# Normalised activations stored with a pair's channels slow and the pixels fast: the first transform of a two-layer convolution kernel loads its weights from consecutive words

## The reference

```python
# layer 0: decorrelated batch normalisation over all 50176 pixels
f  = x_flat - mean                                   # (64, n)
ff = (1 - EPS) * (f @ f.T / (n - 1)) + EPS * eye(64)
L  = cholesky(ff)
out = (solve_triangular(L, eye(64)) @ f) * gamma + beta
# layer 1: Fourier filter block
h = layer_norm(x, n1_g, n1_b)
xf = rfft2(h, axes=(1, 2), norm='ortho')             # 56 x 29 spectrum per channel
# 8 blocks of 8 channels: complex 8x8 product, relu, complex 8x8 product, softshrink
y = irfft2(...)
h = y + h + residual
residual = h
h = gelu(layer_norm(h, n2_g, n2_b) @ mw1 + mb1) @ mw2 + mb2
return h + residual
```

## Time and profile before

| what | value |
|---|---|
| runs of the kernel before | 1067.75, 1069.26, 1069.82 us, median 1069.26 |
| profiled execution, span on the core | 1067.7 us |
| PE / weight load / DVE / ACT / POOL busy | 949.2 / 817.9 / 719.9 / 558.1 / 272.1 us |
| chain that ended last, by engine | PE 57%, DVE 16%, ACT 14%, issue 8%, DMA 4% |

### The profile page before, as it was taken

The page is one execution under the profiler, slowest core; times in us unless marked ns, Lnnn a source line. Parts: engine busy times, 40 slices in busy tenths (PEclk is TensorE's granted clock), DMA queues, the critical chain, the costliest instruction groups (busy, mean ns, idle before and its releaser), DMA issues.

```text
span 1067.7 us, 18451 instructions
## 1 busy us (share of the span) xinstructions
PE 949.2 (89%) x6263; PEld 817.9 (77%) x6263; DVE 719.9 (67%) x2061; ACT 558.1 (52%) x1139; POOL 272.1 (25%) x107
## 2 busy tenths in 40 slices
PE   6989963887999999999999999999998999799787
PEld 6976553685689768976897689768976998499465
DVE  4456786189767776777676767676886688543762
ACT  0002011763776577657765776577647753775333
POOL 2000004034422332233223322332233224230110
PEclk8985565988999999999999999999999999989889
DMA  9922002011000300030003000200000000000001
GB/s 270 261 67 61 1 0 61 1 34 28 1 19 18 83 5 17 17 85 2 17 17 84 3 17 17 87 1 17 17 27 1 19 27 19 0 27 18 18 26 36
DMA packets 9956, 40.78 MB, mean 38 GB/s; under 512 B 1232, under 2 KB 1232, under 8 KB 8208
## 3 DMA queue, kind: packets, MB, share of 16 engines
q1 hardware_dynamic: 9888, 40.00, 13.4%
HBM read 27.15 MB, written 12.85 MB: 37 GB/s over the span
## 4 chain that ended last, share of the span: by engine, by line
PE 57%; DVE 16%; ACT 14%; issue 8%; DMA 4%; DVEq 0%; SPq 0%; ACTq 0%
PE psum L1024 13%; PE psum L909 9%; PE psum L1009 7%; PE psum L962 7%; ACT p_y L1112 7%; ACT o_g L1121 4%; PE psum L943 4%; PE psum L983 4%; PE psum L897 3%; PE psum L836 3%; DMA n<-x_dram 2%; DVE o_g L285 2%; PE psum L884 2%; DVE hbuf L568 2%; DVE stats L527 2%
## 5 line engine op out<-in xcount | busy, mean ns | idle before, releaser
L1153 ACT ACTIVATE hid<-psum,hbias 128x448 f32<-128x448 f32 x224 | 136.2, 634 | 132.2 <-PE psum L1009 131.5
L1024 PEld LDWEIGHTS psum<-prm,hid 128*112 128x112 f32 x1792 | 187.1, 182 | 8.5 <-ACT hid L1153 4.6
L1024 PE MATMUL psum<-prm,hid 128*112 128x96 f32 x1792 | 191.3, 267 | 2.3 <-ACT hid L1153 2.3
L354 POOL TENSOR_TENSOR hbuf<-hbuf,prm 112x1792 f32<-112x1792 f32 x15 | 63.3, 4217 | 328.4 <-DVE hbuf L595 328.4
L644 DVE TENSOR_TENSOR n2T<-psum,n2T 64x448 fp32r<-64x448 f32 x112 | 69.7, 622 | 102.5 <-ACT n2T L1145 101.3
L382 POOL TENSOR_TENSOR p_y<-over,under 116x512 f32<-116x512 f32 x64 | 77.2, 1208 | 201.7 <-ACT under L1171 201.6
L1009 PE MATMUL psum<-n2T,mw1h 128*128 128x448 f32 x224 | 101.8, 455 | 26.4 <-DVE n2T L644 12.8
L909 PEld LDWEIGHTS psum<-cst,hbuf 112*112 112x112 f32 x512 | 99.8, 286 | 20.5 <-issue 19.6
L909 PE MATMUL psum<-cst,hbuf 112*112 112x116 f32 x512 | 99.4, 358 | 18.1 <-DVE hbuf L777 18.1
L962 PE MATMUL psum<-cst,p_y 116*128 116x224 f32 (+1 forms) x480 | 102.1, 356 | 3.0 <-POOL p_y L382 3.0
L1100 ACT COPY u_r<-psum 112x464 f32<-112x464 f32 x64 | 35.0, 547 | 119.8 <-PE psum L909 119.8
(11 more groups left out here) (115 smaller groups left out, 1713.1 us busy)
## 6 DMA issues: line engine op xcount, KB each, us to landing
xin<-x_dram SPq DMA_DIRECT2D x9, 1568.0 KB, 8.9
out_dram<-oslice SPq DMA_DIRECT2D x56, 224.0 KB, 2.2
ybuf<-x_dram SPq DMA_DIRECT2D x2, 1568.0 KB, 18.9
fbuf<-x_dram SPq DMA_DIRECT2D x2, 1568.0 KB, 22.4
n<-x_dram SPq DMA_DIRECT2D x2, 1568.0 KB, 25.5
xin<-x_dram SPq DMA_DIRECT2D x4, 392.0 KB, 5.3
prm<-params_dram SPq DMA_DIRECT2D x1, 771.5 KB, 26.3
cst<-consts_dram SPq DMA_DIRECT2D x1, 652.0 KB, 18.9
```

The lines of the kernel that those rows point to most:

```text
L354: nc.gpsimd.tensor_tensor(h, h, row("b1", WP), ALU.add).then_inc(h_ready, 1)
L1024: last = nc.tensor.matmul(t[0:ROWS, at:at + 96], hid[:, m, w % 2, (w // 2) * ROWS:(w // 2 + 1) * ROWS], pp("mw2")[:, 128 * m + zeros:128 * ...
L1153: nc.scalar.activation(hid[:, q % 2, q // 2, :], ring_c[k % RING_C][:, 0:4 * ROWS], ACT.Gelu, bias=hbias[:, q % 2:q % 2 + 1]).then_inc(c_a ...
```

## The change

The activations of a pixel are kept in the order (j, h) instead of (h, j) in `ybuf`, `rbuf`, `fbuf`, `n2` and `p_y`: channel j stands beside channel 32 + j. `hbuf` alone is turned: (j, w, h), so that `dft_h` reads 112 consecutive numbers. The permutation is brought in by the columns of the whitening matrix `wy` and taken out where `ev_mlp` writes `oslice`; parameters are permuted on the host (`mix`). What reads or writes `hbuf` changes its access pattern:

- `ln1_subtract` reads `ybuf` in order and writes `hbuf` in pairs (h = 0, 1) that lie 448 bytes apart.
- `ln1_rstd`, `ln1_gain` and `bias_h` go through `hbuf` in 32 runs of 56 numbers; their second operand repeats in pairs.
- `residual` on POOL reads `hbuf` in pairs, the other operands in order.
- `ev_mlp` reads `fbuf` with a step of two numbers (8 bytes), 512 numbers each.
- `shrunk_sum` on POOL writes `p_y` with a step of 8 bytes instead of runs of 32 numbers.

```diff
-        h_w = h_nat.rearrange("p (m j) -> p m j", j=CH)
+        h_w = h_nat.rearrange("p (j m) -> p j m", j=CH)
+        h_tok = h_nat.rearrange("p (j w h) -> p w j h", j=CH, h=2)
...
+        def half_h(k):
+            return h_nat.rearrange("p (j w h) -> p j w h", j=CH, h=2)[:, :, k * WP:(k + 1) * WP, :]
+        def row_h(name):
+            return pp(name, ROWS).rearrange("p (j h) -> p j h", h=2).unsqueeze(2).broadcast_to((ROWS, CH, WP, 2))
...
-                        nc.gpsimd.tensor_tensor(h, h, row("b1", WP), ALU.add).then_inc(h_ready, 1)
+                        nc.gpsimd.tensor_tensor(h, h, row_h("b1"), ALU.add).then_inc(h_ready, 1)
...
-                    nc.gpsimd.tensor_tensor(r3, h3, y3, ALU.add).then_inc(r_ready, 1)
+                    nc.gpsimd.tensor_tensor(r4, h_tok, y4, ALU.add).then_inc(r_ready, 1)
...
-                        yk = y_v[0:2 * KR, 4 * k:4 * k + L2_KP[k], :].rearrange("p k (m h j) -> p h k m j", h=2, j=CH)[:, half]
+                        yk = y_v[0:2 * KR, 4 * k:4 * k + L2_KP[k], :].rearrange("p k (m j h) -> p h k m j", h=2, j=CH)[:, half]
...
-                    link(nc.vector.tensor_copy(wy[0:C, 0:C], wt_ps))
-                    link(nc.vector.tensor_copy(wy[C:2 * C, C:2 * C], wt_ps))
+                    for v in range(2):
+                        link(nc.vector.tensor_copy(
+                            wy[C * v:C * v + C, C * v:C * v + C].rearrange("p (j h) -> p h j", h=2),
+                            wt_ps.rearrange("p (h j) -> p h j", h=2)))
...
                 def ln1_subtract(i, k):
-                    subtract_mean(ybuf, h_nat, 0, k)
+                    ws = slice(k * WP, (k + 1) * WP)
+                    nc.vector.tensor_tensor(h_tok[:, ws], ybuf[:].rearrange("p (w j h) -> p w j h", j=CH, h=2)[:, ws],
+                                            small[:, 0, ws].unsqueeze(2).unsqueeze(2).broadcast_to((ROWS, WP, CH, 2)),
+                                            ALU.subtract).then_inc(norm_step[0], 1)
                 def ln1_rstd(i, k):
-                    multiply_rstd(h_nat, i, 0, k).then_inc(norm_step[0], 1)
+                    dve.wait_ge(norm_step[0], norm_count(i, 0, 2 * k + 1))
+                    nc.vector.tensor_tensor(half_h(k), half_h(k),
+                                            small[:, 3, k * WP:(k + 1) * WP].unsqueeze(1).unsqueeze(3).broadcast_to((ROWS, CH, WP, 2)),
+                                            ALU.mult).then_inc(norm_step[0], 1)
...
-                    return nc.vector.tensor_tensor(half_w(h_nat, k), half_w(h_nat, k), row("g1", WP), ALU.mult)
+                    return nc.vector.tensor_tensor(half_h(k), half_h(k), row_h("g1"), ALU.mult)
...
-                    nc.vector.tensor_tensor(oslice[:, s % 2, :], ring_c[k % RING_C][0:ROWS, :],
-                                            fbuf[:, s * SW * C:(s + 1) * SW * C], ALU.add).then_inc(c_dve, 1)
+                    nc.vector.tensor_tensor(
+                        oslice[:, s % 2, :].rearrange("p (w h j) -> p w h j", h=2, j=CH),
+                        ring_c[k % RING_C][0:ROWS, :].rearrange("p (w h j) -> p w h j", h=2, j=CH),
+                        fbuf[:, s * SW * C:(s + 1) * SW * C].rearrange("p (w j h) -> p w h j", h=2, j=CH),
+                        ALU.add).then_inc(c_dve, 1)
...
-                            last = nc.tensor.matmul(t[0:ROWS, j * 2 * KR:(j + 1) * 2 * KR], h_w[:, :, 4 * k + j],
+                            last = nc.tensor.matmul(t[0:ROWS, j * 2 * KR:(j + 1) * 2 * KR], h_w[:, 4 * k + j, :],
                                                     cc("f1", ROWS), start=True, stop=True)
```

More of the change, by code:

```diff
@@ L344, in _ @@
                 nc.gpsimd.memset(u_r[:], 0.0).then_inc(s_ones, 1)
-                h3, y3, r3, f3 = (t.rearrange("p (w c) -> p w c", c=C) for t in (h_nat, ybuf[:], r_nat, fbuf[:]))
+                f3 = fbuf[:].rearrange("p (w c) -> p w c", c=C)
+                y4, r4 = (t.rearrange("p (w j h) -> p w j h", j=CH, h=2) for t in (ybuf[:], r_nat))
                 def bias_h(i):
                     for k in range(1 if first(i) else 2):
-                        h = h3[:, k * WP:(k + 1) * WP]
+                        h = half_h(k)
                         pool.wait_ge(n1_ready, i * 2 + k + (1 if first(i) else 0))
-                        nc.gpsimd.tensor_tensor(h, h, row("b1", WP), ALU.add).then_inc(h_ready, 1)
+                        nc.gpsimd.tensor_tensor(h, h, row_h("b1"), ALU.add).then_inc(h_ready, 1)
                 def residual(i):
@@ L776, in first_h @@
                     dve.wait_ge(h0_step, 1)
-                    nc.vector.tensor_tensor(half_w(h_nat, 1), half_w(h_nat, 1), row("b1", WP), ALU.add).then_inc(h0_half, 1)
+                    nc.vector.tensor_tensor(half_h(1), half_h(1), row_h("b1"), ALU.add).then_inc(h0_half, 1)
                 covariance_and_factor()
@@ L1304, in rows, with mix @@
         return np.broadcast_to(v.reshape(1, -1), (128, v.size))
+    def mix(v):
+        return v.reshape(2, CH, -1).transpose(1, 0, 2).reshape(v.shape)
     G = CH // BS
@@ L1321, in layout @@
     put("w2", a.reshape(128, -1))
-    put("mw1", np.tile(i["L1_conv_mw1"], (2, 1)))
+    put("mw1", np.tile(mix(i["L1_conv_mw1"]), (2, 1)))
     m = np.zeros((HH, 2, 128), np.float32)
@@ L1325, in layout @@
     put("mw2", m)
[L1326 to L1329, removed]
+    put("beta", rows(mix(i["L0_conv_beta"])))
+    put("g1", rows(mix(i["L1_conv_n1_g"])))
+    put("b1", rows(mix(i["L1_conv_n1_b"])))
+    put("mb2", rows(mix(i["L1_conv_mb2"])))
     fb2 = i["L1_conv_b2"].reshape(2, 2, CH).transpose(1, 0, 2)
@@ L1332, in layout @@
     put("gamma", i["L0_conv_gamma"].reshape(C, 1))
-    put("g2", np.tile(i["L1_conv_n2_g"], 2).reshape(128, 1))
-    put("b2", np.tile(i["L1_conv_n2_b"], 2).reshape(128, 1))
+    put("g2", np.tile(mix(i["L1_conv_n2_g"]), 2).reshape(128, 1))
+    put("b2", np.tile(mix(i["L1_conv_n2_b"]), 2).reshape(128, 1))
     fb1 = i["L1_conv_b1"].reshape(2, 2, CH).transpose(0, 2, 1)
```

## The result

The changed kernel took 1029.9 us in the median of 4 runs (1024.93 to 1037.10), the kernel before 1069.5 (1067.75 to 1071.48): a ratio of 0.9632 with a 95% interval of 0.9591 to 0.9674. The profiled execution is the slowest of the four: its span is 1035.2 us. It lost 4.5 us before the first row transform (start at 183.85 instead of 179.32): the covariance's loads, where the change does nothing, left it 5.8 us late, of which it got 1.3 back. From there to the end it is 37.0 us shorter than the one of before.

What follows compares the result with a forecast made beforehand. PE bounds the step, busy 100.92 of 106.52 us. Gains of 2.8 (pair 0), 3 x 5.5 and 4 x 4.0 make 35.3; 1069.3 - 35.3 + 1.2 (clock) = 1035.2, predicted 1035, range 1024 to 1048.

Steps and rivals of the forecast that it cites:

- The load is what makes the stage long, and the stage is on the path: Row transform on PE: weight loads fall from 286 to about 180 ns, the 12.23 us stage lying wholly on the path.
- The spacing: Row transform's matmuls: 105.5 ns each instead of 191, bounds 98 to 110, saving 5.5 us per pair.
- Pair 0: First pair's row transform: nothing saved in the half at low clock, 2.8 us saved in the rest.
- DVE gives back in pairs 2 to 5 and not in 1, 6 and 7: PE's wait before mlp grows to about 2.7 us; pairs 2 to 5 gain 4.0 us each, the others 5.5.
- The patterns cost nothing: New access patterns on DVE and POOL: operations keep their times, a gain excluded; upper end on hbuf 1.1 us each.
- The rule on adjacent pairs: Skill page's rule: hbuf pairs free, single words in ev_mlp cost 0.35 us; as rival 7 us, 1042, chance 0.15 or 0.08: 0.08.
- The clock: Before mlp in pairs 2 to 5: half a fall, 1.2 us; rival of several falls, 1044, chance 0.15.

Runs made afterwards that it cites:

- pe_only: Kernel before, only the row transform changed to read consecutive numbers from the unturned hbuf (wrong numbers transformed): 1033.5 us, ratio 0.9681.
- patterns_only: Changed kernel, its row transform reading with a step of 32 numbers again, the new patterns on DVE and POOL kept: 1064.7 us, ratio 0.9977.
- late_load: Changed kernel, the input load of pair i+2 issued only when ACT has evicted the row transform of pair i: 1018.3 us, ratio 0.9557.
- single_words: Changed kernel, DVE's first normalising operation going through h before j, writing hbuf in single words 448 bytes apart: 1041.4 us, ratio 0.9760.

## Why the prediction was right, point by point

- *The load is what makes the stage long, and the stage is on the path.* Right, and shown by `pe_only` and `patterns_only`, which split the change: 0.968 and 0.998.
- *The spacing.* Predicted 105.5 ns on the line between L1024's 98 and L897's 110; measured 99, inside the bounds but near the lower. So the stage saved 5.9 instead of 5.5 us, 2.8 us more over seven pairs if all of it were kept. The straight line between L1024 and L897 was the weak step: L897's 110 ns come from 8 matmuls alone. Why the transform lies so near to L1024 no run separates.
- *Pair 0.* Predicted 2.8, measured 12.57 - 9.52 = 3.05 in the stage and 3.9 in the step. At the low clock nothing was saved, as assumed: 6.35 us for 33 matmuls before, 6.06 for 31 after, 192 and 196 ns each. That the size fits is partly luck, since it hangs on when the clock rises: in the second profile of the changed kernel the stage takes 8.70 us.
- *DVE gives back in pairs 2 to 5 and not in 1, 6 and 7.* Right: PE's wait grew from 1.32 to 2.49 us in those four (I had put 2.7), and was 1.32 and 1.17 in pairs 1 and 6. Without a fall of the clock these steps gained 4.2 and 4.7, where I had 4.0. `late_load` shows the cause: with DVE's issue time down from 6.3 to 2.0 us each step keeps 6.0 us. Two things I had otherwise. The loss has a second place, the wait of `whiten` for `ev_whiten` (0.83 us in pair 2, 0.48 in pair 4). And what DVE gives back isn't fixed: it follows the issue time one for one. Wherever the clock held, a step's gain and DVE's issue time in it add up to the same: 4.2 + 6.67 and 4.7 + 6.18 here, 5.1 + 5.68 and 3.9 + 6.97 in the second profile, 10.8 to 10.9 us each time. In `pe_only` they add up to 10.7, which is the patterns' 0.14.
- *The patterns cost nothing.* Right for all: 2.03, 2.02 (the median, which leaves the two beside POOL's bias out) and 2.03 us on `hbuf`, 687 ns for `ev_mlp`, POOL's `residual` 7.84. What I excluded, a gain, exists on POOL, 0.8 us an operation, but is worth only 0.14 us a step.
- *The rule on adjacent pairs.* Of the Trainium skill's section "Measured stream behaviour on trn2" (Vector Engine (DVE) Microarchitecture Reference) this case shows one half: pairs that hop are free (2026 ns), single words that hop cost 0.71 ns each (3297). The other half it doesn't bear out: a source stepping by 8 bytes costs nothing (`ev_mlp`, 687 ns against 689 before). `ev_mlp` also reads PSUM, at 1.3 ns an element against the 1.13 of `hbuf`'s operations, which could hide a part of such a price; but L505 reads no PSUM and shows none either. In `single_words` the source steps by 8 bytes as well, so that its 0.71 ns are the price of both together. My weighing of L505 against the rule held.
- *The clock.* I allowed half a fall, 1.2 us, and said that rows can't tell. The profile has two at the place I named, 2.2 and 3.3 us of gain left in those steps. With the issue times of these pairs (7.00 and 6.34) the sum above would have left 3.9 and 4.5 at full clock, so the falls cost 1.6 and 1.2 us, below my 2.5 to 3.4, since the clock was down for 3.4 us and not for 6.8. A second profile of the changed kernel has two as well, in pairs 2 and 5 (1.3 and 1.2 us). Which pair is hit differs between two profiles of one kernel, with the same wait of 2.49 us before it in pairs without a fall.

Sum of the profile: 3.9 + 5.9 + 14.4 + 6.1 + 6.7 = 37.0 us against the 34.1 I had forecast with the clock in. Pair 0 gave 1.1 more, pairs 1, 6 and 7 together 2.2 more. Pairs 2 to 5 gave 14.4 against my 14.8, where two errors met: gains larger than I had put, and two falls of the clock for the half that I had. The rest of the way to 1029.9 is the spread of the runs (12 us from the fastest to the slowest), of which the part ahead of the first transform moved the profiled one by 4.5 us.

What exactly DVE waits for at its loop's end the waits don't name, but the DMA packets in the traces nearly do. In every one of these waits there is one packet of 8 KB on the instruction queue q14 behind which DVE starts (times in us):

| profile, pairs | DVE's wait | from the wait's start to the packet's | from its landing to DVE's start |
|---|---|---|---|
| before, 2 to 5 (load running) | 6.5 to 7.0 | 4.3 to 4.8 | 1.7 |
| changed, 2 to 5 (load running) | 6.2 to 7.0 | 4.0 to 4.8 | 1.7 to 1.8 |
| changed, 6 (no load) | 2.0 | 0.1 | 1.4 |
| `late_load`, 2 to 6 (load later) | 2.0 to 2.2 | 0.1 | 1.5 to 1.6 |

So DVE starts at a nearly fixed time after that packet, and with the load under way the packet comes some 4 us later. That it holds DVE's own instructions, and that it queues behind the load's packets, is still argued: the trace names neither the packet's engine nor what delays it.

## What to carry to other kernels

A stationary operand should be read with a step of at most 8 bytes in float32: with 16 to 128 bytes a matmul took twice as long here (191 to 209 ns against 99), whatever the distance. The reordering was free since its other readers and writers on DVE keep pairs of adjacent words or step by 8 bytes; a single word that hopped cost DVE 0.7 ns. When a stage on one engine gets shorter, measure on the others how much idle time lies ahead of the place that it next waits for: here 4.1 us of slack turned a gain of 5.9 into 3.9 to 5.1, and one wait that moved a load by 8 us gave the rest back, in all 11 us, with an edit that was worth nothing in the kernel before.

## What the runs showed of the hardware that was not expected

- Weights read with a step of 16 or 32 bytes take 206 to 209 ns a matmul, more than with 64 or 128 bytes (192, 191).
- POOL adds two tensors in 1.8 ns an element when the second operand repeats a pair of words (3.22 us for 1792), and in 2.2 when it runs through 64 words (4.01 us, medians of the lines); a hopping first operand (`residual`, 7.84 us for 3584) changes nothing.
- At the turn of its hardware loop DVE waited 5.7 to 7.6 us while a load of 1568 KB was running, in all profiles, and 2.0 to 2.3 us without it. With the load the 8 KB instruction packet came 3.5 to 5.4 us into the wait, without it 0.1 to 0.4 us.
